# Attention scores from two float32r parts in 32-row tiles instead of three bf16 parts

## The reference

```python
q = x @ Wq
latent_kv = (x @ Wk + x @ Wv) @ W_down_kv
k_rec, v_rec = latent_kv @ W_up_k, latent_kv @ W_up_v        # 16 heads of 8
scores = einsum('bhqd,bhkd->bhqk', qh, kh) / sqrt(128)
decay = exp(-0.01 * 0.01 * abs(i - j))                        # scores are multiplied by it
attn = softmax(clip(clip(scores) * decay))
x = layernorm(x + (attn @ vh) @ Wo)
x = layernorm(x + experts(x) + shared(x))
```

## Time and profile before

| | us |
|---|---|
| median of three runs | 857.0 |
| span of the profiled execution | 854.4 |
| what the median holds beside that span (857.0 - 854.4) | 2.6 |
| prologue, until the first scores | 0 to 72.4 |
| attention, until the table load that follows the last exponential | 72.4 to 603.4 |
| experts | 603.4 to 854.4 |

### The profile page before, as it was taken

One profiled execution on the slowest core, in us unless ns is written; L12 is line 12 of the kernel. 1 busy time (PEld: TensorE's weight loads), 2 busy tenths in 40 slices (PEclk: granted clock), 3 DMA queues, 4 the chain that ended last, 5 costly groups with the idle time before them and its releaser, 6 DMA issues. The chain is left out here.

```text
span 854.4 us, 15303 instructions
## 1 busy us (share of the span) xinstructions
PE 796.4 (93%) x4889; PEld 338.1 (40%) x4889; DVE 426.2 (50%) x1237; ACT 581.9 (68%) x687; POOL 279.3 (33%) x182
## 2 busy tenths in 40 slices
PE   6546899999999999999999999999999999999996
PEld 4321233333332333333323333333565656666564
DVE  3962434344333333333333333334487777867874
ACT  4444799999999999999999999998422222221221
POOL 5929929939900000000000000000245444544443
PEclk9787999999999999999999999999999999999999
DMA  5222232233231111111111111150000000000000
GB/s 170 75 100 100 119 141 107 112 140 125 95 138 80 80 79 80 80 79 76 71 73 75 68 74 74 72 162 13 2 1 26 22 4 25 25 0 25 12 1 25
DMA packets 26101, 60.38 MB, mean 71 GB/s; under 512 B 1568, under 2 KB 17376, under 8 KB 21472
## 3 DMA queue, kind: packets, MB, share of 16 engines
q1 hardware_dynamic: 23680, 50.69, 15.8%
q0 software_dynamic: 2400, 9.44, 2.7%
HBM read 45.44 MB, written 14.68 MB: 70 GB/s over the span
## 5 line engine op out<-in xcount | busy, mean ns | idle before, releaser
L519 ACT ACTIVATE probs<-ps 128x1024 f32<-128x1024 f32 x480 | 464.3, 1022 | 47.4 <-DVE ps L894 39.1
L894 DVE TENSOR_TENSOR ps<-ps,cpk 128x128 f32<-128x128 f32 x512 | 152.5, 299 | 308.9 <-PE ps L642 279.3
L642 PE MATMUL ps<-stacks 128*128 128x512 bf16 (+3 forms) x1408 | 270.0, 325 | 19.4 <-DMA stacks<-parts_dram 15.3
L657 PE MATMUL ps<-probs,Vring 128*32 128x512 f32 x2048 | 273.6, 606 | 0.5 <-ACT probs L524 0.5
L642 PEld LDWEIGHTS ps<-stacks 128*128 128x128 bf16 x1408 | 110.3, 98 | 298.0 <-issue 176.5
L541 ACT ACTIVATE stacks<-ps 128x512 f32<-128x512 f32 x80 | 47.8, 597 | 184.9 <-PE ps L627 184.9
L427 POOL TENSOR_TENSOR small<-small 128x4 f32<-128x4 f32 x8 | 8.2, 1022 | 347.8 <-DVE small L862 347.8
L444 POOL TENSOR_TENSOR stacks<-stacks 128x512 f32<-128x512 f32 x64 | 81.7, 1276 | 59.3 <-DVE stacks L1002 58.6
L626 PE MATMUL ps<-stacks,stage 128*128 128x512 f32 x160 | 82.0, 594 | 0.0
L627 PE MATMUL ps<-stacks,stage 128*128 128x512 f32 x160 | 81.7, 592 | 0.0
L749 PEld LDWEIGHTS ps<-stage,stacks 128*128 128x128 f32 x512 | 65.0, 191 | 41.3 <-issue 27.6
(11 more groups left out here) (105 smaller groups left out, 510.0 us busy)
## 6 DMA issues: line engine op xcount, KB each, us to landing
stacks<-parts_dram SPq DMA_DIRECT2D x192, 192.0 KB
parts_dram<-stage POOLq DMA_DIRECT2D x6, 1536.0 KB, 14.9
parts_dram<-stage SPq DMA_DIRECT2D x4, 768.0 KB, 3.5
probs<-in_L_attn_x SPq DMA_DIRECT2D x4, 512.0 KB, 4.8
ptmp<-in_L_attn_x SPq DMA_DIRECT2D x8, 256.0 KB, 3.2
out<-stacks SPq DMA_DIRECT2D x8, 256.0 KB, 2.4
rows_sb<-in_decay_rows SPq DMA_DIRECT2D x2, 512.0 KB, 6.5
stage<-in_L_ffn_fc_w SPq DMA_DIRECT2D x1, 1024.0 KB, 8.4
```

Of the source, the lines that this page charges most:

```text
L519: nc.scalar.activation(probs[:, m % 6, :], slot[m % 3], ACT.Exp, scale=SCALE).then_inc(score_slots_free, 1)
L642: last = mm(slot[m % 3][:, lo:hi], sv[:, u, 1, h, v, kt * P:(kt + 1) * P], sv[:, u, 0, h, v, lo:hi], start=True, stop=True)
L657: last = mm(bank[6][r:r + 32, :], Vring[:, u, kt, h, :], probs[:, (2 * g + h) % 6, qh * HALF:(qh + 1) * HALF], start=(kt == 0), stop=(kt = ...
L894: tt(d, d, diag_fix, ALU.mult).then_inc(diag_done, 1)
```

## The change

NPART becomes 2, and a part is float32r (4 bytes) instead of bf16. The split takes three operations instead of five, on both engines. A head's products take 2 x 2 x 8 = 32 rows; the two heads of a pair lie in rows 0 to 31 and 32 to 63, and each is a row tile of TensorE of its own. A score tile now holds two heads x 512 queries: each head writes its own PSUM bank of the slot. The matmuls a pair remain 44. The diagonal is fixed in 8 of a pair's 16 tiles, 128 x 2 x 128 elements at once, and ScalarE waits for `scores_ready` in the others. The zero rows and their memsets go. `load_pair` issues eight DMAs of 2 x 8 rows of 8 KB. The experts' buffers move from `stacks` to `qT`, `kT` and the rest of `stage`.

```diff
-NPART = 3
+NPART = 2
...
-    parts_dram = nc.dram_tensor("parts_dram", (2, NPART, B * P, 2 * S), BF16, kind="Internal").ap()
+    parts_dram = nc.dram_tensor("parts_dram", (2, NPART, B * P, 2 * S), F32, kind="Internal").ap()
...
-        stacks = sb("stacks", [P, 3 * 2 * 2 * 2 * S], BF16)
-        sv = stacks[:, :].rearrange("r (u k h v s) -> r u k h v s", u=3, k=2, h=2, v=2)
+        stacks = sb("stacks", [2 * HROWS, 3 * 2 * 2 * S], F32R)
+        sv = stacks[:, :].rearrange("r (u k v s) -> r u k v s", u=3, k=2, v=2)
...
-                for a in range(NPART):
-                    rows = slice(a * NPART * HD, (a + 1) * NPART * HD)
-                    q_part = parts_dram[0, a:a + 1, here, :].rearrange("a (d h) s -> a d (h s)", h=2)
-                    k_parts = parts_dram[1, :, here, :].rearrange("b (d h) s -> b d (h s)", h=2)
-                    for n, src in ((0, q_part.to_broadcast([NPART, HD, 4 * S])), (1, k_parts)):
-                        dst = sv[rows, u, n, :, :, :].rearrange("r h v s -> r (h v s)")
-                        sp.dma_start(dst, src).then_inc(stack_loaded[u], 16)
+                for h in range(2):
+                    q_parts, k_parts = (parts_dram[n, :, here, :].rearrange("a (d h) s -> h a d s", h=2)[h] for n in range(2))
+                    for a in range(NPART):
+                        rows = slice(h * HROWS + a * NPART * HD, h * HROWS + (a + 1) * NPART * HD)
+                        for n, src in ((0, q_parts[a:a + 1].to_broadcast([NPART, HD, 2 * S])), (1, k_parts)):
+                            sp.dma_start(sv[rows, u, n, :, :].rearrange("r v s -> r (v s)").bitcast(F32), src).then_inc(stack_loaded[u], 16)
...
+                nc.gpsimd.tensor_tensor(lo, f, hi.bitcast(F32), ALU.subtract).then_inc(pool_chain, 1)
...
-            for u in range(1, 3):
-                nc.gpsimd.memset(sv[64:P, u].rearrange("r k h v s -> r (k h v s)").bitcast(F32), 0.0).then_inc(pads_zeroed, 1)
...
-                    cuts = sorted({0, kt * P, HALF, S})
+                    q0, q1 = qh * HALF, (qh + 1) * HALF
+                    cuts = sorted({q0, min(max(kt * P, q0), q1), q1})
                     for lo, hi in zip(cuts, cuts[1:]):
                         v = 0 if lo >= kt * P else 1
-                        last = mm(slot[m % 3][:, lo:hi], sv[:, u, 1, h, v, kt * P:(kt + 1) * P], sv[:, u, 0, h, v, lo:hi],
-                                  start=True, stop=True)
+                        for h in range(2):
+                            rows = slice(h * HROWS, (h + 1) * HROWS)
+                            last = mm(slot[m % 3][:, h * HALF + lo - q0:h * HALF + hi - q0], sv[rows, u, 1, v, kt * P:(kt + 1) * P],
+                                      sv[rows, u, 0, v, lo:hi], start=True, stop=True)
...
+                    if not on_diagonal(m):
+                        return
                     dve.wait_ge(scores_ready, i * TPB + (m + 1))
-                    d = slot[m % 3][:, kt * P:(kt + 1) * P]
-                    tt(d, d, diag_fix, ALU.mult).then_inc(diag_done, 1)
+                    at = kt % CT * P
+                    d = slot[m % 3].rearrange("j (h q) -> j h q", h=2)[:, :, at:at + P]
+                    tt(d, d, diag_fix.unsqueeze(1).to_broadcast([P, 2, P]), ALU.mult).then_inc(diag_done, 1)
```

More of the change, by code:

```diff
@@ L28 @@
 F32 = mybir.dt.float32
+F32R = mybir.dt.float32r
 BF16 = mybir.dt.bfloat16
@@ L74, in block_kernel @@
     NE = E + gate_w.shape[1] // F
+    HROWS = NPART * NPART * HD
     SCALE = float(np.float32(1.0) / (np.sqrt(np.float32(D)) + np.float32(1e-8)))
@@ L143, in block_kernel @@
         x_tok = probs[:, 0:B, :]
-        gflat = stacks[:, :].bitcast(F32)
+        gflat = stage[:, :, :, :].rearrange("p k a s -> p (k a s)").bitcast(F32)
         g_qk = gflat[0:HD, 0:4 * S].rearrange("d (k h s) -> d k h s", k=2, h=2)
@@ L152, in block_kernel @@
         NB = HALF
-        ev = [gflat[:, n * NB:(n + 1) * NB] for n in range(22)]
+        spare = NE * (2 * F + D)
+        ev = [t[:, n * NB:(n + 1) * NB] for t in (qT, kT) for n in range(8)]
+        ev += [late[:, spare + n * NB:spare + (n + 1) * NB] for n in range(8)]
         x_res = [ptmp[:, 0, q * NB:(q + 1) * NB] for q in range(2)]
@@ L365, in split @@
                 tab = rows_sb[:, v ^ n, 0:tokens]
-                hi, mid, lo = (stage[:, n, a, v * S:v * S + tokens] for a in range(NPART))
-                f, r = ptmp[:, 0, 0:tokens], ptmp[:, 1, 0:tokens]
+                hi, lo = (stage[:, n, a, v * S:v * S + tokens] for a in range(NPART))
+                f = ptmp[:, 0, 0:tokens]
                 nc.gpsimd.tensor_tensor(f, src, tab, ALU.mult).then_inc(pool_chain, 1)
@@ L389, in _ @@
             for v, tokens in ((0, S), (1, K_SHARE)):
-                split(kT[:, 0:tokens], 1, v, v * 5, tokens)
+                split(kT[:, 0:tokens], 1, v, v * 3, tokens)
                 pool.sem_inc(stage_ready[1], 1)
@@ L401, in _ @@
                         for v in range(2):
-                            split(qkT[n][:, bass.ds(b * S, S)], n, v, b * 20 + (n * 10 + v * 5 - 10))
+                            split(qkT[n][:, bass.ds(b * S, S)], n, v, b * 12 + (n * 6 + v * 3 - 6))
                             apart(pool)
                         pool.dma_start(parts_dram[n, :, bass.ds(b * P, P), :].rearrange("a r s -> r a s"),
-                                       stage[:, n, :, :]).then_inc(pool_stored[n], 16)
+                                       stage[:, n, :, :].bitcast(F32)).then_inc(pool_stored[n], 16)
                     for n in range(2):
@@ L823, in _ @@
                     dve.wait_ge(s_rows, 32)
-                    hi, mid, lo = (stage[:, n, a, v * S + t0:(v + 1) * S] for a in range(NPART))
-                    f, r = probs[:, 4, t0:S], probs[:, 5, t0:S]
+                    hi, lo = (stage[:, n, a, v * S + t0:(v + 1) * S] for a in range(NPART))
+                    f = probs[:, 4, t0:S]
                     link(tt(f, qkT[n][:, t0:S], rows_sb[:, v ^ n, t0:S], ALU.mult))
                     link(nc.vector.tensor_copy(hi, f))
-                    link(tt(r, f, hi, ALU.subtract))
-                    link(nc.vector.tensor_copy(mid, r))
-                    link(tt(lo, r, mid, ALU.subtract))
+                    link(tt(lo, f, hi.bitcast(F32), ALU.subtract))
                     dve.sem_inc(stage_k_rest if n else stage_ready[0], 1)
```

34 lines of the change are left out of this document (16 added, 18 removed).

## The result

The changed kernel takes **989.7 us** (median of four runs, 988.6 to 991.6) against 856.8 us for the kernel before in the same session: a ratio of 1.155, with a 95% interval of 1.1535 to 1.1563. That is 133 us slower; 127 were forecast.

A forecast was written before the change was run, and what follows sets the result against it. Stack loads were taken to bound attention: 47.5 (first issue) + 2.5 (latency) + 32 x 19.7 + 29.5 (stores) = 709, plus 22 (end), 251.0 (experts) and 2.6 outside the span: 984 us, range 955 to 1025.

The forecast's parts named there:

- to the first matmul: Start of attention: from the first load's issue, 2.5 us of latency and 19.7 us for the first pair's stacks.
- 31 further pairs: Attention after the first pair: loading paces every pair to the last, at 19.7 us each.
- GpSimd's stores: Six stores of 2 MB on all engines, also the two that load: loading loses 29.5 us in all.
- experts' weights: Weights and rows of x queue behind the last stack loads; plus 2 us at attention's end for the rows of x.
- end of attention: From the last pair's stacks to attention's end: 19.9 us before, less 1, plus 1.5 (clock), plus 2; together 22 us.
- Two engines, 19.7 us a pair: Stack loads: the source's outer count of 2 leaves two engines, 53.3 GB/s, 19.7 us a pair; chance 0.83.
- Prologue: Splits ahead of attention: fewer operations, last split ends at 43.3 us, first load issued at 47.5 instead of 55.07.
- The waits: Sign in attention: TensorE waits for the stacks once a pair, some 4 us or more, 31 or 32 times.
- Score matmuls: TensorE's float32r scores: 0.5 us a group instead of 0.97; anything up to 1.4 us stays hidden under loading.
- What lies around the span: Outside the profiled span: the median exceeds it by 2.6 us, added to the span of 982.
- The faster one: Rival on stack loads: they spread or keep their rate, 13.1 to 2.7 us a pair; 798 or 788 us; chance 0.10.
- The slow matmuls: Rival on float32r scores: 2.05 us a group, 24.9 us a pair, 1132 us in all; chance 0.05.

The follow-up runs named there:

- E1: Changed kernel with the stack loads' source walked dimension first, part second (8 x 2 rows instead of 2 x 8), same bytes and DMAs: 800.1 and 800.5 us.
- E4: E1 with each stack load cut into two of 4 x 2 rows, sixteen DMAs a pair instead of eight: 806.7 us.
- E6: E1 with each load DMA writing every second of a head's 32 partitions instead of 16 neighbouring ones: 800.4 us, ratio 0.936 to the kernel before.
- E5: E1 with the score matmuls as float32 instead of float32r: 1106.2 us.
- E7: E6 with 14 unread bf16 matmuls on TensorE ahead of the first score tile: median 797.2 us, ratio 0.926 to the kernel before.
- E2: Kernel before (3 bf16 parts) with its stack loads walked dimension first, 8 x 3 rows instead of 3 x 8: 843.9 us, ratio 0.987.

## Why the prediction was right, step by step

| term | forecast | measured | from |
|---|---|---|---|
| first load issued | 47.5 | 48.2 | SyncE's timeline |
| to the first matmul | 22.2 | 22.7 | 70.96 - 48.22 |
| 31 further pairs | 610.7 | 611.3 | 31 x 19.72 |
| GpSimd's stores | 29.5 | 29.9 | 199.47 - 70.96 - 5 x 19.72 |
| experts' weights | none | 2.7 | 714.98 - 672.86 - 2 x 19.72 |
| end of attention | 22 | 24.0 | 738.93 - 714.98 |
| experts | 251.0 | 251.0 | 989.9 - 738.9 |
| span | 982 | 989.9 | |

The rows behind these, from SyncE's, TensorE's, ScalarE's and VectorE's timelines of the changed kernel:

```profile
43.65 0.42 DVE L834 TENSOR_TENSOR stage<-probs,stage 128x256 fp32r<-128x256 f32 x1
...
48.22 112.14 SPq L295 DMA_DIRECT2D stacks<-parts_dram  x46
...
70.96 1.75 PE L650 MATMUL ps<-stacks 32*128 32x512 f32 x8 [19.63 <-DMA stacks<-parts_dram]
...
199.47 0.79 PE L650 MATMUL ps<-stacks 32*128 32x512 f32 x2 [5.45 <-DMA stacks<-parts_dram]
...
672.86 0.79 PE L650 MATMUL ps<-stacks 32*128 32x512 f32 x2 [4.97 <-DMA stacks<-parts_dram]
...
714.98 0.79 PE L650 MATMUL ps<-stacks 32*128 32x512 f32 x2 [4.31 <-DMA stacks<-parts_dram]
...
738.93 1.28 ACT L546 ACT_TABLE_LOAD   x1
```

The forecast's terms add up to 983 and not 982; the recorded sum dropped the fraction.

*Two engines, 19.7 us a pair.* Right to 0.1%: 19.72. The step that a share of 0.19 means three engines, and that two parts leave two, was an inference from one number; E1, E4 and the changed kernel now show shares of 0.49, 0.25 and 0.13, that is 8, 4 and 2 engines, for outer counts of 8, 4 and 2.

*Stores.* 29.9 us for 29.5. The stores share the two engines, as reckoned.

*Prologue.* The last split ends at 43.65 + 0.42 = 44.1 against 43.3, the issue follows 0.7 late.

*Experts' weights.* This was missed. The prediction put the weights behind the last loads on the queue and took them as harmless to those. But they run while the last pair is loading, and at a share of 0.71 they must use the two engines of the stacks too. The window shows it, and the same interval of two pairs is 42.1 us instead of 39.4:

```profile
690.00:700.00 10.00, 9.97 (x78) 3.45 (x74) 3.31 (x8) 9.65 (x11) 0.00 (x0) 0.97 0.71 180
```

*End of attention.* 24.0 instead of 22. The term "1.5 us for the clock" was too small: from 715 to 720 the granted clock is 0.50 and from 720 to 730 it is 0.59, while the row after a similar idle of before, on which the term rested, had 0.79 over 4 us.

*The waits.* Forecast were 31 or 32 waits of 4 us or more; 22 are put down to the stacks, 15 of them of 4 us or more and four under 1 us. The step that failed is that every pair computes at full clock. The time that the forecast has TensorE wait in each pair is in truth spent, in about every second pair, on slower work at 1.2 GHz. Since loading sets the pace either way, this moved no time except in the last pair.

*Score matmuls.* Forecast 0.5 us a group at the pace of bf16; 0.66 us, and more where a tile is cut at the diagonal. Under the limit of 1.4, so still hidden.

*What lies around the span.* 2.6 us were added; in the profiled run it is 991.6 - 989.9 = 1.7, and that run is the longest of the four, 1.9 above the median. So the sum was short by 7.9 us in the span, and by 5.7 in the end.

*The rivals.* The faster one asked whether the queue's rate could be its own limit; E1 and E6 show 111 and 184 GB/s on the same queue, so it is not. Its time, 798 with ScalarE as the bound, is near what E1 gives (800) once the loads do spread. Its lower end, 2.7 us a pair, left out the cap by partitions that E1 ran into: its first pair took 11.9 us from the first issue. The slow matmuls are E5, at 1106 against the 1132 worked out for the changed kernel with its later start.

What stays open is why the granted clock returns so late behind a wait. E7 shows that a clock brought up ahead of the scores does not stay up.

## What to carry to other kernels

Look for a DMA share that is constant while its queue always has work: in this case a share of k sixteenths was a load on k engines, and the order of the source's dimensions, not the bytes, set k. The rate was k times 26.7 GB/s with two and three engines; with four (at first) and eight it stayed below that, held by the partitions that a DMA writes. When a change alters an outer count (parts, heads, a broadcast), work out the time of a transfer again at the new count, and compare it with the compute time that used to cover it; here the margin was 1.5 us in 16.25. Reordering the dimensions of the source cost nothing that shows and was worth 189 us; the rest of the change was worth 44.

## What the runs showed of the hardware that was not expected

- More engines do not give a rate in proportion if the DMA writes few groups of four neighbouring partitions. Two engines had 53 GB/s. Four had 53 into 8 partitions (E4, its first windows), and eight had 111 into 16 (E1), 168 into 24 (E2) and 184 into 16 spread over 32 (E6).
- VectorE's copy of a pair's values (128 x 128 elements) takes 0.22 us in most pairs, but up to 5.47 us while GpSimd splits parts: 5.47 in the profile of before, 4.79 in that of the changed kernel, 4.27 in E7's. In all three it is 0.22 us in every pair after GpSimd's last split (stored by 234 us before, by 176 us in the other two). In the changed kernel it cost nothing, as TensorE still had to wait 7.23 us for the stacks of a later pair, until 150.29; before and in E7 TensorE idled for 3.53 and 2.56 us behind it. What decides how long a copy takes while GpSimd splits, no run shows.
- Behind a wait of 4 us TensorE stayed at 1.2 GHz for some 10 us of gapless work in row tiles of 32 (396.7 to 407), and in E1 from 54 to about 81 us, with no gap from 64.8 on. In E5, with float32 scores, it was 0.50 from 58 to 116 us, with TensorE busy without a gap from 59.5 on, and 1.00 from 118 us on with the same work. In the kernel before, whose scores use 72 rows of 128, it was back by about 77 us behind the first wait, which ended at 72.36. Which property of the work matters, no run separates. The windows, first of the kernel before, then of E1:

```profile
76.00:78.00 2.00, 2.00 (x14) 0.54 (x13) 0.59 (x2) 2.00 (x3) 2.00 (x2) 0.84 0.17 74
78.00:80.00 2.00, 2.00 (x16) 0.65 (x15) 0.60 (x2) 1.76 (x3) 1.92 (x2) 1.00 0.20 86
```

```profile
74.00:80.00 6.00, 6.00 (x28) 1.70 (x28) 1.02 (x3) 3.88 (x4) 5.74 (x4) 0.50 0.59 212
80.00:86.00 6.00, 5.98 (x45) 2.01 (x43) 2.06 (x6) 5.43 (x6) 4.77 (x3) 0.91 0.34 119
```

- float32r matmuls of 32 x 512 are single instructions, and four of them, two heads side by side, take 0.66 us at 2.4 GHz; as float32 they are two instructions each and take 1.93 us.
